# Pre-norm attention with a mixture of experts: A ahead of M with the first scores, a list level for the last three token tiles, and two chunks' sums behind the last gate

## What is computed

```python
x = L0_attn_in_features                                    # (4, 1024, 128)
n = layernorm(x)
q, k, v = n @ w_q.T, n @ w_k.T, n @ w_v.T                  # w_*: (1024, 128), one head of 1024
att = softmax(causal(q @ k.T / sqrt(1024)))
x = x + (att @ v) @ w_o.T                                  # w_o: (128, 1024)
h = layernorm(x)
scores = softmax(h @ gate_w.T)                             # 8 experts
top, sel = top_k(scores, 2)
y = sum over the 2 choices of  top * (silu(h @ w1[e]) * (h @ w3[e])) @ w2[e]     # 128 -> 256 -> 128
out = x + y
```

## Time and profile before

| | us |
|---|---|
| median of 3 runs | 240.25 (239.41 to 241.43) |
| the profiled execution | 239.77 |
| its span, first to last instruction | 238.0 |
| TensorE busy | 227.5 |
| VectorE busy | 185.9 |
| GpSimd busy | 162.1 |
| ScalarE busy | 145.8 |

### The profile page before, as it was taken

One profiled execution on the slowest core, in us unless ns is written; L12 is line 12 of the kernel. 1 busy time (PEld: TensorE's weight loads), 2 busy tenths in 40 slices (PEclk: granted clock), 3 DMA queues, 4 the chain that ended last, 5 costly groups with the idle time before them and its releaser, 6 DMA issues.

```text
span 238.0 us, 6499 instructions
## 1 busy us (share of the span) xinstructions
PE 227.5 (96%) x1814; PEld 209.2 (88%) x1815; DVE 185.9 (78%) x848; ACT 145.8 (61%) x391; POOL 162.1 (68%) x204
## 2 busy tenths in 40 slices
PE   7989999999999999999999999989999999999973
PEld 6978888898799767877999999979999999999973
DVE  2479898879897789977898799757666666699955
ACT  2267787777877757755599665646565656565200
POOL 6513327888888888868577777777777777777500
PEclk9999999999999999999999999999999999999999
DMA  6999800111111111115134426533433434598474
GB/s 229 310 321 332 226 4 28 43 37 45 34 50 35 48 34 47 45 37 136 37 70 107 114 82 145 137 92 101 105 112 91 106 95 108 183 342 266 121 266 134
DMA packets 31947, 28.89 MB, mean 121 GB/s; under 512 B 4137, under 2 KB 26545, under 8 KB 31921
## 3 DMA queue, kind: packets, MB, share of 16 engines
...
q0 software_dynamic: 4096, 8.53, 10.6%
...
...
## 4 chain that ended last, share of the span: by engine, by line
PE 79%; POOL 6%; DMA 4%; issue 3%; DVE 3%; ACT 2%; POOLq 1%; DVEq 0%; SPq 0%
PE scores L727 12%; PE turned L727 12%; PE scores L598 12%; PE weighed L654 11%; PE scores L748 6%; PE turned L624 5%; POOL expert_rows L505 4%; PE mixed L748 3%; PE weighed L748 3%; PE mixed L613 3%; PE mixed L612 3%; DMA XX<-choice_rows 2%; DVE X L1369 2%; PE scores L744 2%; DMA TL<-L_attn_w_o 1%
## 5 line engine op out<-in xcount | busy, mean ns | idle before, releaser
L505 POOL DMA_INDIRECT expert_rows<-rows,slots x64 | 64.5, 1008 | 18.2 <-issue 12.6
L516 POOL DMA_INDIRECT choice_rows<-ysb,ycol x64 | 63.6, 993 | 19.5 <-issue 10.7
L865 ACT ACTIVATE Wt<-W 128x512 f32 x71 | 44.1, 624 | 15.7 <-issue 15.7
L727 PE MATMUL scores<-xT,Wt 128*128 128x128 f32 x288 | 38.3, 276 | 1.1 <-issue 1.1
L598 PE MATMUL scores<-XX,TL 128*128 128x512 f32 (+3 forms) x96 | 38.1, 506 | 0.2 <-ACT TL L838 0.2
L654 PE MATMUL weighed<-TL,PT 128*128 128x136 f32 x272 | 37.0, 281 | 0.8 <-DVE X L989 0.7
L727 PE MATMUL turned<-xT,Wt 128*128 128x128 f32 x280 | 37.1, 275 | 0.0
L727 PEld LDWEIGHTS scores<-xT,Wt 128*128 128x128 f32 x288 | 35.0, 192 | 1.4 <-issue 1.4
L654 PEld LDWEIGHTS weighed<-TL,PT 128*128 128x128 f32 x272 | 33.7, 190 | 1.7 <-issue 1.6
L727 PEld LDWEIGHTS turned<-xT,Wt 128*128 128x128 f32 x280 | 34.1, 192 | 0.0
L977 DVE TENSOR_REDUCE negmax<-scores 128x1 f32<-128x128 f32 (+7 forms) x32 | 23.5, 734 | 4.9 <-PE scores L598 4.9
...
## 6 DMA issues: line engine op xcount, KB each, us to landing
...
XX<-choice_rows SPq DMA_DIRECT2D x16, 256.0 KB, 4.0
...
expert_rows<-rows,slots POOLq DMA_INDIRECT x64, 2.5
choice_rows<-ysb,ycol POOLq DMA_INDIRECT x64, 2.3
...
```

The lines of the kernel that those rows point to most:

```text
L505: nc.gpsimd.indirect_dma_start(xs, bass.IndirectOffsetOnAxis(ap=slots[:, u, k:k + 1], axis=0), rows[:, u % ROWS_RING, k, :], None).then_in ...
L516: nc.gpsimd.indirect_dma_start(yb, bass.IndirectOffsetOnAxis(ap=ycol[:, q, 0:1].bitcast(u32), axis=0), ysb[:, q, :], None).then_inc(y_out[ ...
L727: mm(bank[2 + j % RING][:, c * P:(c + 1) * P], Wt[:, j % RING, c * P:(c + 1) * P], xT[:, j % RING, :], start=True, stop=True)
L865: copy(Wt[:, j % RING, :], W[:, ds(w * (SET // WIDE), SET)], ACT.Copy).then_inc(Wt_rdy, 1)
```

## The change

- **Start.** w_q and w_k are issued before w_o and w_v. TensorE makes A first, then the queries of four tiles (AHEAD_Q) apart from their values, the transposes of w_o, the first scores, M, MT and MG among the first turned probabilities, and then four tiles' values; `out_query` and `out_values` copy them out apart. The loops start at slot 2. Six warm-up products in one place take the place of 13 in two. The statistics run 10 tiles ahead for 12. woT and MT lie in Wt.
- **List.** A fourth level: the counts before the last three token tiles (SOWN). SEG is 32 for 24. So 65 row tiles are stored for 64, and six are sown for seven, into three token tiles for four. `ranks` and `places` take one more count in the last group. `clear` is gone; the first product of a bank starts it.
- **End.** `yf` has eight places, in the memory of TL. Chunks 0 to 2 are added inside the tiles, 3 to 6 behind the last gate (`N_SOON`). Chunk 7 is fetched when all 65 stores have landed, one choice by SP and one by ScalarE; it is added in four halves after the sown rows. `pair` comes before `sow` in the last tiles. GpSimd's stores from tile 48 on are unrolled.

```diff
 NT0 = (ROWS_HALF - E * (P - 1)) // P // LANES * LANES
 NEAR = 16
-FAR, LATER = 6, 64
-LEVELS = (HALF, FAR, len(GROUPS) - 1)
+FAR, LATER = 6, 63
+SOWN = 3
+LEVELS = (HALF, FAR, len(GROUPS) - 1, len(GROUPS) - 1)
 SEG = len(LEVELS) * E
 NT1 = LISTED - NT0
 assert (ROWS_HALF + E * (P - 1)) // P - NT0 <= NEAR
 assert (K * P * sum(n for _, n in GROUPS[:FAR + 1]) + E * (P - 1)) // P <= LATER
+assert GROUPS[-1][1] > SOWN
...
 NF = N_TILES // FIN
-ZF = 4
+ZF = 8
 CHUNKS = [(0, 2), (4, 4), (6, 4), (12, 4), (14, 4), (20, 4), (22, 4), (28, 2)]
 N_EARLY, N_LATER = 5, 7
 FETCH_AT = [66, 67, 68, 69, 70]
-ADD_AT = [59, 61, 62, 64, 65]
+N_SOON, ADD_AT = 3, [59, 61, 63]
+REST_OF = (STORED // OUT_LANES, STORED % OUT_LANES)


 def pieces(c):
@@ -98,8 +101,9 @@
...
-STAT1_GROUP, STAT1_EARLY = 4, 12
-WARM, WARM_ON = 5, 8
+STAT1_GROUP, STAT1_EARLY = 4, 10
+WARM = 6
+AHEAD_Q = 4
 NORM1_LEAD, NORM1_BY_DVE = 4, 8
 PV_LAG, X1_LAG, NORM2_LAG = 1, 2, 3
...
-            sp.dma_start(wo_sb, w_o).then_inc(wo_in, 16)
             H2 = HALF_QT // 2
             sp.dma_start(Xv[:, 0, 0:HALF_QT, :], xv[:, 0, 0:HALF_QT, :]).then_inc(x_head, 16)
-            sp.dma_start(wv_sb, w_v.rearrange("(p c) i -> p c i", p=P)).then_inc(wv_in, 16)
             wqv, wkv = (w.rearrange("(p c) i -> p c i", p=P) for w in (w_q, w_k))
             for c, arrived in ((0, wqk_lo_in), (FC // 2, wqk_hi_in)):
                 sp.dma_start(wq_sb[:, c:c + FC // 2, :], wqv[:, c:c + FC // 2, :]).then_inc(arrived, 16)
                 sp.dma_start(wk_sb[:, c:c + FC // 2, :], wkv[:, c:c + FC // 2, :]).then_inc(arrived, 16)
+            sp.dma_start(wo_sb, w_o).then_inc(wo_in, 16)
+            sp.dma_start(wv_sb, w_v.rearrange("(p c) i -> p c i", p=P)).then_inc(wv_in, 16)
             for i, arrived in ((0, x_next), (H2, x_mid)):
                 for b, j in ((0, HALF_QT + i), (1, i)):
                     sp.dma_start(Xv[:, b, j:j + H2, :], xv[:, b, j:j + H2, :]).then_inc(arrived, 16)
             sp.dma_start(Xv[:, 1, HALF_QT:, :], xv[:, 1, HALF_QT:, :]).then_inc(x_tail, 16)
-            sp.dma_start(Xv[:, 2, :, :], xv[:, 2, :, :]).then_inc(x_tail, 16)
+            sp.dma_start(Xv[:, 2, :, :], xv[:, 2, :, :]).then_inc(x_more, 16)
             sp.dma_start(Xv[:, 3, :, :], xv[:, 3, :, :]).then_inc(x_far, 16)
             for half, w in enumerate((w1, w3)):
                 sp.dma_start(We[:, :, half * H:(half + 1) * H], w.rearrange("e p h -> p e h")).then_inc(w_in, 16)
...
+            for c in range(N_SOON):
                 write(c)
-            for q in range(OUT_LANES):
-                sp.wait_ge(y_out[q], 16 * len(range(q, LATER, OUT_LANES)))
-            for c in range(N_EARLY, NF):
+            stores_in(sp, 0, LATER)
+            for c in range(N_EARLY, LAST):
                 fetch(c)
-
-            sp.wait_ge(sum2, 1)
-            n, z = pieces(LAST)[0]
-            sp.dma_start(ov[:, n:n + z, :], X[:, n:n + z, 0:D]).then_inc(out_done, 16)
+            stores_in(sp, LATER, STORED)
+            fetch_last(sp, 0)
+            write_last(sp, 0)
             sp.wait_ge(out_done, 16 * sum(len(pieces(c)) for c in range(NF)))


...
                     store(r, q)
+            for t in range((REST_OF[0] - 1) * OUT_LANES, STORED):
+                store(t // OUT_LANES, t % OUT_LANES)


         @block.tensor
...
-                       start=True, stop=False)
-
             def sow(t):

                 n = t - STORED
                 pe.wait_ge(y_rdy, t + 1)
                 pe.wait_ge(pick_rdy, n + 1)
-                for i in range(FIN):
-                    o = mm(ACC[i // 2][:, i % 2 * D:(i % 2 + 1) * D], pick[n][:, i * P:(i + 1) * P], ysb[:, t % OUT_LANES, :],
-                           start=False, stop=n == BY_PE - 1 and i % 2 == 1)
-                    if n == BY_PE - 1 and i % 2 == 1:
-                        o.then_inc(sown_mm, 1)
+                for i in range(SOWN):
+                    a, at = sown_at(i)
+                    o = mm(a[:, at:at + D], pick[n][:, i * P:(i + 1) * P], ysb[:, t % OUT_LANES, :],
+                           start=n == 0 and at == 0, stop=n == BY_PE - 1, skip_group_check=True)
+                if n == BY_PE - 1:
+                    o.then_inc(sown_mm, 1)
...
+            pe.wait_ge(wqk_lo_in, 32)
+            for c in range(FC):
+                if c == FC // 2:
+                    transposes(-XT_LEAD)
+                    pe.wait_ge(wqk_hi_in, 32)
+                i = mm(pS[0][:, 512:512 + P], wq_sb[:, c, :], wk_sb[:, c, :], start=c == 0, stop=c == FC - 1)
+            i.then_inc(A_mm, 1)
+            transposes(1 - XT_LEAD)
+            pe.wait_ge(A_rdy, 1)
+            query(0)
+            transposes(2 - XT_LEAD)
+            query(1)
             pe.wait_ge(wo_in, 16)
             wo_c = wo_sb.rearrange("p (q c) -> p c q", c=FC)
             for c in range(FC):
                 nc.tensor.transpose(pT[c // 4][:, c % 4 * P:(c % 4 + 1) * P], wo_c[:, c, :],
                                     identf[:, :]).then_inc(woT_mm, 1)
-            for _ in range(WARM_ON):
-                mm(pM[:, 0:P], identf[:, :], identf[:, :], start=True, stop=True)
+            pe.wait_ge(consts, N_CONST)
+            scores(0)
+            query(2)
+            transposes(3 - XT_LEAD)
+            scores(1)
+            query(3)
             pe.wait_ge(wv_in, 16)
+            pe.wait_ge(gwT_rdy, 1)
             pe.wait_ge(woT_lo_rdy, 1)
             for c in range(FC):
                 if c == FC // 2:
                     pe.wait_ge(woT_hi_rdy, 1)
-                i = mm(pS[1][:, 0:P], wv_sb[:, c, :], woT[:, c, :], start=c == 0, stop=c == FC - 1)
+                i = mm(pO[:, 2 * P:3 * P], wv_sb[:, c, :], woT[:, c, :], start=c == 0, stop=c == FC - 1)
...
+            turn(0)
+            pe.wait_ge(M_rdy, 1)
+            nc.tensor.transpose(pO[:, P:2 * P], M_sb[:, 0:P], identf[:, :]).then_inc(MT_mm, 1)
+            turn(1)
             pe.wait_ge(MT_rdy, 1)
             mm(pO[:, 0:E], MT, M_sb[:, VG:], start=True, stop=True).then_inc(MG_mm, 1)
-            transposes(1 - XT_LEAD)
-            pe.wait_ge(A_rdy, 1)
+            scores(2)
+            pe.wait_ge(tl_ev, AHEAD_Q)
             pe.wait_ge(MG_rdy, 1)
-            pe.wait_ge(consts, N_CONST)
+            for u in range(AHEAD_Q):
+                values(u)
+            transposes(1)
+            weigh(0)
...
-                sow(t - 2)
                 pair(*divmod(t + LAG, LANES), w[LIST0 + t % LANES])
+                if t - 2 >= STORED:
+                    sow(t - 2)
             sow(NT - 2)
             sow(NT - 1)

...
+            out_xx(-XT_LEAD)
+            act.wait_ge(A_mm, 1)
+            copy(A_sb[:, :], pS[0][:, 512:512 + P], ACT.Copy, scale=float(F_ATT) ** -0.5).then_inc(A_rdy, 1)
+            out_xx(1 - XT_LEAD)
+            out_query(0)
+            out_xx(2 - XT_LEAD)
+            out_query(1)
+            act.wait_ge(woT_mm, FC)
+            copy(woT[:, FC // 2:, :].rearrange("p c q -> p (c q)"), pT[1][:, :], ACT.Copy).then_inc(woT_hi_rdy, 1)
+            out_query(2)
+            exps(0)
+            out_xx(3 - XT_LEAD)
+            out_query(3)
+            exps(1)
+            act.wait_ge(M_mm, 1)
+            copy(M_sb[:, 0:P], pO[:, 2 * P:3 * P], ACT.Copy).then_inc(M_rdy, 1)
+            out_pt(0)
+            act.wait_ge(MT_mm, 1)
+            copy(MT, pO[:, P:2 * P], ACT.Copy).then_inc(MT_rdy, 1)
+            out_pt(1)
+            exps(2)
+            for u in range(AHEAD_Q):
+                out_values(u)
+            out_xx(1)
+
+            for s in range(2, LAST_SLOT + 1):
                 if s == N_TILES:
                     act.wait_ge(list_rdy, 1)
...

-            for c in range(N_EARLY, N_LATER):
+            stores_in(act, 0, STORED)
+            fetch_last(act, 1)
+            for c in range(N_SOON, N_LATER):
                 act.wait_ge(sum1, c + 1)
                 for n, z in pieces(c):
                     act.dma_start(ov[:, n:n + z, :], X[:, n:n + z, 0:D]).then_inc(out_done, 16)
-            act.wait_ge(sum2, 2)
-            n, z = pieces(LAST)[1]
-            act.dma_start(ov[:, n:n + z, :], X[:, n:n + z, 0:D]).then_inc(out_done, 16)
+            write_last(act, 1)


         @block.vector
...
-                    link(v.tensor_tensor(cnt[:, LEVELS.index(gr), :], RANKS[0:1, n * E:(n + 1) * E], stretch0[0:1, :],
+                    link(v.tensor_tensor(cnt[:, NL - 1 if gr == NG - 1 else LEVELS.index(gr), :],
+                                         RANKS[0:1, n * E:(n + 1) * E], stretch0[0:1, :], ALU.subtract))
+                if gr == NG - 1:
+                    link(v.tensor_tensor(cnt[:, NL - 2, :], RANKS[0:1, (n + 1) * E:(n + 2) * E], stretch0[0:1, :],
                                          ALU.subtract))
                 v.tensor_tensor(picked[:, gr % 2, 0:n, :, :], hot[:, a:a + n, :, :],
                                 RANKS[:, 0:n * E].rearrange("p (a e) -> p a e", a=n).unsqueeze(2).to_broadcast([P, n, K, E]),
...
```

(55 more changed lines are left out.)

158 lines of the change are left out of this document (76 added, 82 removed).

## The result

| | before | after | forecast |
|---|---|---|---|
| median, us | 240.84 of 4 | 244.56 of 4 | 242.0 |
| lowest to highest | 239.41 to 241.63 | 242.88 to 245.22 | 237.7 to 243.8 |
| ratio | | 1.0173 [1.0131, 1.0214] | |
| profiled execution, span | 239.77, 238.0 | 245.15, 243.4 | 241.5, 239.8 |

What follows compares the result with a forecast made beforehand. TensorE was taken as the bound, with 79% of the chain that ended last. Start +1.7, list +1.3 and tail -1.25 sum to +1.75, so 240.25 becomes 242.0 us; range 237.7 to 243.8.

Steps and rivals of the forecast that it cites:

- Landing of w_k, 7.5: Start: with 1.25 MB ahead of A's end, the weights A needs land at 7.5 us; bounds 6.4 and 8.3.
- my upper bound of 8.3: Start: the latest landing allowed for the weights A needs, against an estimate of 7.5 us.
- forecast 12.45: Start: TensorE begins M's 16 records at 12.45 us and ends them at 14.25.
- From M to slot 2, 7.35: Start: M begins at 12.45 and slot 2 opens at 19.8, behind ScalarE's eight value copies and XX of tile 4.
- forecast 1.7: Start: slot 2 opens at 19.8 us against 18.08, +1.7, and the shift goes through whole.
- The clock: Start: the sum without the throttling rule keeps +1.7; with a late rise of TensorE's clock the start comes to +3.2.
- a rival with the price 1.5: Start: TensorE's clock stays at its lower level through A and w_o's turning, +1.5, 243.5 us; 0.18 together with the tail rival.
- the end's: Tail rival: the end gives nothing as chunk 5's fetch lands 1.2 late, 243.2 us; 0.18 together with the clock rival.
- Attention, 0: Between slot 2 and the experts: `STAT1_EARLY` 10 stays behind TensorE's work, so no cost.
- List, +1.3: Expert tiles where the list is made: VectorE's longer passes make TensorE wait, +1.3 us; bounds 0.2 and 1.7.
- the lower bound's reason: List: only 0.2 us if stalls there are won back from the 1.05 at the loop's jump.
- End, -1.25: Tail: last gate ends at 225.0 and VectorE at 234.4 against 235.64, -1.25 us; bounds -2.0 and +0.5.

Runs made afterwards that it cites:

- r8: The changed kernel with 17 warm-up products in one row for six, and w_q and w_k each in one transfer: one execution 242.43 us, before's median 239.82.
- r14: The changed kernel with 13 warm-up products for six, and three more between A's halves: ratio 1.0139 to before, on a slower chip.
- r17: r14 with ScalarE's XX copy of tile 4 behind two pairs of value copies instead of four: 241.72 us, ratio 1.0056 to before.
- r3: The same kernel as r14 (changed kernel, 13 warm-up products and three more between A's halves): ratio 1.0117 to before, on a slower chip.
- r13: The changed kernel with the first norm's statistics 12 tiles ahead for 10: ratio 1.0194 to before, on a slower chip.
- r4: The kernel before without the eight warm-up products between the transposes of w_o and M: ratio 0.9982 to before.
- r9: The kernel before with the first norm's statistics 10 tiles ahead instead of 12: ratio 0.9996 to before, on a slower chip.
- r6: The kernel before with the list's fourth level alone: pair(3) to pair(32) 44.81 us, for 43.88 in the kernel before.
- r18: Before's start with the changed list and end, the list's parts spread behind tiles 4, 5, 6, 9, 12, 15, 18: 238.86 us, ratio 0.9936 to before.

## Why the forecast was wrong, point by point

- **Landing of w_k, 7.5.** It was 8.47, past my upper bound of 8.3. I had taken the rate of four transfers in before and added "some for the smaller pieces". Per transfer the pieces took 5.0 (the first half of w_k) and 5.7 (the second), r8's whole w_k 5.3 and was there at 7.1. The term was mis-sized by 1.0. With the clock kept it moved M by 0.8 (13.29 in r14, forecast 12.45).
- **From M to slot 2, 7.35.** Right: 7.03, with ScalarE's row as its last link (r17). The order of the start, with the clock kept, costs 2.3 (20.58 less 18.27, means), or 2.5 against this before's 18.08; forecast 1.7.
- **The clock.** The step that failed. The sum had the chain run at the upper level; that it does not was a rival with the price 1.5 and, with the end's, 0.18. r3, r14 and r8 show it to be the largest term: 2.7 to 3.0 where the clock falls from 8.0 to 14.9, 2.0 where it rises late (22.31 in r13, 20.30 in r14, on one chip). My reason against it, that TensorE had been fed for 2.7 us before the gap, was half true: it did rise by 6.85 in after, and then fell again. I had priced only a late rise, eight plus 12 records at 0.1, which is 2.0 and not the 1.5 that I wrote; the late rise of r13 cost those 2.0. A fall behind the gap was not among my cases. The Trainium skill's page "TensorE: Matmul & The Clock Gate", section "What's actually happening", says the throttled state is the default and that activity releases it. The traces agree in that the level rose, or came back, only behind fed time in after, r13 and r4. A gap of 1.95 to 2.17 us lies ahead of both falls and of r13's late rise, and no profiled start without such a gap had the fall; a late rise came without one too (r9, no gap above 0.43).
- **Attention, 0.** It cost 0.4 on this kind of chip. I had written that `STAT1_EARLY` 10 stays behind TensorE's work, without looking where GpSimd's last power of four would fall among the scatters.
- **List, +1.3.** The mechanism was right, VectorE's backlog seen at tiles 16 to 22, +1.14 at pair(23); then 0.5 came back at the jump, which I had named as the lower bound's reason. +0.7 in after, 0.9 in r6.
- **End, -1.25.** The last gate I had at 225.0; less the shift of pair(66) it was 225.1. VectorE's end I had at 234.4; it was 234.06. So -1.58, in r18 whole, in after -1.0 since its last write took 0.6 longer.
- **Sum.** Order +2.5 (the fed starts' 20.58 less this before's 18.08), clock +2.7 (23.32 less 20.58), attention +0.4, list +0.7, end -1.0: +5.3 of the 5.4 of the profiled pair. The medians lie 3.7 apart. After's profiled execution has a mean granted clock of 0.979: its fall at the start takes off 0.014, and one behind TensorE's last product, where nothing waits for the clock, the rest. The other three have 0.989, 0.989 and 0.997 and spans of 242.2, 243.4 and 241.1. The one with 0.997 can't have had that fall, and the two with 0.989 hardly the whole of it; a late rise would not show in this column. They weren't profiled. So not every execution has the profiled start, and part of the profiled pair's difference need not be in the medians.
